# The first gathering layer of a four-layer graph network: 16 row buffers, one-hot tables three pairs ahead, group sums in pairs of one bank, the block stage over two parts

## The reference, cut to what matters

```python
x = _layernorm(x + _L0_gnn_ref(x, src, dst, edge_weight, kernel, bias))   # weighted scatter
x = _layernorm(x + _L1_gnn_ref(x, bases, weights, src, dst, edge_type_64)) # the layer of this change
x = _layernorm(x + _L2_gnn_ref(x, edge_index, edge_type_2, ...))          # 2 edge types
x = _layernorm(x + _L3_gnn_ref(x, edge_index, W1, b1, W2, b2))            # 2 convolutions

def _L1_gnn_ref(x, bases, weights, source, target, edge_type):
    xs = x[source]
    alpha = weights[edge_type]                     # 8 numbers an edge
    m = sum(alpha[:, b:b+1] * (xs @ bases[b]) for b in range(8))
    return segment_sum(m, target, num_segments=6250)
```

## Time and profile before

| what | us |
|---|---|
| median of 3 runs | 4323.59 |
| lowest and highest | 4319.92, 4335.91 |
| span of the profiled execution | 4355.4 |
| of it pass 1, first gather to last product | 1264.1 |
| busy in pass 1: PE, DVE, POOL, ACT | 780.9, 538.6, 802.9, 112.9 |

### The profile page before, as it was taken

One profiled execution on the slowest core, in us unless ns is written; L12 is line 12 of the kernel. 1 busy time (PEld: TensorE's weight loads), 2 busy tenths in 40 slices (PEclk: granted clock), 3 DMA queues, 4 the chain that ended last, 5 costly groups with the idle time before them and its releaser, 6 DMA issues. The chain is left out here.

```text
span 4355.4 us, 78937 instructions
## 1 busy us (share of the span) xinstructions
PE 3123.5 (72%) x19042; PEld 2324.3 (53%) x19043; DVE 2245.6 (52%) x6922; ACT 1982.0 (46%) x2698; POOL 2898.9 (67%) x2439
## 2 busy tenths in 40 slices
PE   4777877777777771565666666666888887887887
PEld 3444544444444440344444444445777777887877
DVE  7877777777777775344444444444022323223223
ACT  3555565555655553000001000103666666766665
POOL 3888888888888887666666666664655553553554
PEclk7888788887888885677777777777988998998898
DMA  8555666655655657111111111112444446766665
GB/s 283 99 101 101 108 112 111 106 103 104 116 101 98 108 102 246 44 47 47 48 51 49 48 48 51 49 48 71 128 137 139 138 136 186 217 212 200 203 198 155
DMA packets 362034, 506.40 MB, mean 116 GB/s; under 512 B 58808, under 2 KB 260748, under 8 KB 361324
## 3 DMA queue, kind: packets, MB, share of 16 engines
q0 software_dynamic: 178752, 183.65, 24.5%
q1 hardware_dynamic: 130122, 230.91, 17.6%
q10 hardware_dynamic: 52898, 89.11, 5.6%
HBM read 336.75 MB, written 170.10 MB: 116 GB/s over the span
## 5 line engine op out<-in xcount | busy, mean ns | idle before, releaser
L978 POOL DMA_INDIRECT rows<-t,idx_ring x1184 | 1141.7, 964 | 716.1 <-issue 329.3
L1686 PE MATMUL bank<-arena 128*128 128x384 bf16 (+1 forms) x2496 | 682.0, 409 | 397.5 <-DVE arena L2374 300.1
L1022 POOL DMA_INDIRECT sums<-rows,idx_ring x416 | 666.7, 1603 | 143.5 <-issue 115.1
L1022 POOL DMA_INDIRECT sums<-stage,idx_ring x416 | 667.2, 1604 | 126.9 <-issue 100.4
L1553 PE MATMUL bank<-planes,x_sides 128*128 128x256 f32 x3920 | 578.9, 302 | 72.2 <-issue 58.9
L978 POOL DMA_INDIRECT rows<-xp,idx_ring x384 | 373.3, 972 | 376.7 <-DMA xp<-alpha 114.3
L1553 PEld LDWEIGHTS bank<-planes,x_sides 128*128 128x128 f32 x3920 | 528.1, 204 | 84.5 <-issue 74.0
L1424 PE MATMUL bank<-S,rows 128*128 128x192 f32 x1664 | 514.4, 446 | 0.6 <-issue 0.6
L1121 ACT ACTIVATE node_data<-bank,most_sb 128x408 f32 x720 | 391.4, 602 | 229.5 <-PE bank L1689 201.5
L1686 PEld LDWEIGHTS bank<-arena 128*128 128x128 bf16 x2496 | 174.6, 109 | 599.6 <-issue 452.4
L2373 DVE TENSOR_SCALAR arena<-S 128x1176 bf16<-128x1176 int16 x832 | 450.0, 541 | 0.5 <-issue 0.5
(11 more groups left out here) (266 smaller groups left out, 5083.6 us busy)
## 6 DMA issues: line engine op xcount, KB each, us to landing
adj<-node_data ACTq DMA_DIRECT2D x112, 448.0 KB
rows<-adj SPq DMA_DIRECT2D x102, 448.0 KB
bases_sb<-adj SPq DMA_DIRECT2D x65, 448.0 KB
arena<-src SPq DMA_DIRECT2D x104, 256.0 KB
rows<-t,idx_ring POOLq DMA_INDIRECT x1184
adj_even<-node_data ACTq DMA_DIRECT2D x77, 224.0 KB
S<-adj SPq DMA_DIRECT2D x36, 448.0 KB
arena<-type SPq DMA_DIRECT2D x52, 256.0 KB
```

What stands on the lines that cost most here:

```text
L978: nc.gpsimd.indirect_dma_start(out=(part_rows if p > 2 else rows)[:, k, t, :], out_offset=None, in_=row_tables[p], in_offset=bass.Indirect ...
L1022: nc.gpsimd.indirect_dma_start(out=sums_t[t], out_offset=bass.IndirectOffsetOnAxis(ap=idx4[:, k, t:t + 1], axis=0), in_=msg[k][:, t, :], i ...
L1686: nc.tensor.matmul(bank[bk][:, 0:(hb - ha) * W], lo, hw_hot[n * GT + t][:, ha * W:hb * W], start=t == 0, stop=False)
```

## The change

In pass 1 only:

- **Rows.** The ring has 16 buffers: the old eight (`rows`) for the first body of a part and eight in `shared` (`rows_late`) for the second. POOL waits for the products of group g−16. `idx_ring` still holds two bodies and is copied where it was.
- **One-hot tables.** Four `S` buffers, made three pairs ahead.
- **Sums.** Two groups share a bank, so that four banks hold eight groups. PE waits for a free bank and DVE for the products once a pair (for the pair's second group).
- **Stage.** `base_piece` moves from pair 0 to pair 3, `add_piece` from pair 2 to pair 4. The stage takes two parts: TURN and RESIDUAL at pair 6 and NORM at pair 7 of the part three later, TURN_ROWS at pair 2 and PROJECT and TABLE at pair 4 of the part after that. The last steps of half-block NH−3 move behind the loop.
- **Around it.** The first two typed loads move from ahead of the pass to behind its last product; ACT's turning of them is split over TURN and NORM of the last half-block. `x1_back` is folded into `stored0`.

```diff
 PRODUCTS_AHEAD = RING
+ROWS_AHEAD = 2 * RING
 ADDED_AHEAD = 2
 SUM_RING = (0, 1, 3, 6)
+SUM_SLOTS = 2 * len(SUM_RING)
+S1_RING, S1_AHEAD = 4, 3
 
 STEPS = 17
 HSTEPS = BPH * RING // 2
 TURN, RESIDUAL, NORM, TURN_ROWS, PROJECT, TABLE = 5, 6, 7, 8, 10, 11
...
-PLACES = {1: {3: (TURN,), 4: (RESIDUAL,), 5: (NORM,), 6: (TURN_ROWS,), 7: (PROJECT, TABLE, REST, MID, LOW)},
-          2: {}}
-PIECE_DONE, PIECE_ADDED = 0, 2
+FIRST_HALF = {6: (TURN, RESIDUAL), 7: (NORM,)}
+SECOND_HALF = {2: (TURN_ROWS,), 4: (PROJECT, TABLE)}
+PIECE_DONE, PIECE_ADDED = 3, 4
 HB = -(-N // P)
 HW_COLS = HB * W
...
+        S_of = [S[:, 0, :, :], S[:, 1, :, :], late_S[:, 0, :, :], late_S[:, 1, :, :]]
+        rows_late = shared[:, :, :, :, :].rearrange("p e s t f -> p (e s t f)").rearrange("p (k t f) -> p k t f", k=RING, t=GT)
+        rows1 = (rows, rows_late)
+        assert len(S_of) == S1_RING == PAIRS and SUM_SLOTS == RING
         rows4 = rows[:, :, :, :].rearrange("p (s h) t f -> p s (h t) f", h=FHALF)
         sel = [shared[:, 0, s, :, :] for s in range(2)]
...
 
-        def sums_bank(k):
-
-            return bank[SUM_RING[k % len(SUM_RING)]]
+        def sums_at(k):
+
+            return bank[SUM_RING[k // 2]][:, k % 2 * (NB * W):(k % 2 + 1) * (NB * W)]
 
         def count_at(k):
 
-            return sums_bank(k)[0:2, BC - W:BC]
+            at = BC - (2 - k % 2) * W
+            return bank[SUM_RING[k // 2]][0:2, at:at + W]
 
         def parts_of(e, k, part):
...
 
             sp.wait_ge(adj_stored, 16 * NPC * (NCHUNK + 1))
             sp.wait_ge(ohot_ready, NG)
-            for m in range(2):
-                load_typed(m)
             with sp.Fori(0, NH - 2) as b:
                 sp.wait_ge(rows_ready[1], b + 2)
                 sp.dma_start(half_rows(t2_pairs, b), hst[1][0][:, 0:HALF * 2 * P].rearrange(
                     "p (c f) -> p c f", c=HALF)).then_inc(stored[1], 16)
+            sp.wait_ge(products[1], ROWS_AHEAD + NG)
+            for m in range(2):
+                load_typed(m)
             sp.wait_ge(based, NPT)
             for m in range(2, PIECES2):
...
-                                    out=(part_rows if p > 2 else rows)[:, k, t, :], out_offset=None, in_=row_tables[p],
+                                    out=(part_rows if p > 2 else rows1[j] if p == 1 else rows)[:, k, t, :], out_offset=None,
+                                    in_=row_tables[p],
                                     in_offset=bass.IndirectOffsetOnAxis(ap=idx_ring[:, j, k, t:t + 1], axis=0),
-                                ).then_inc(gathered[k], 16)
+                                ).then_inc((gathered1[j] if p == 1 else gathered)[k], 16)
 
             def gather_general(p, flag):
...
 
-                if b == NH - 3 and at == TURN_ROWS:
-                    act.wait_ge(s_ready[1], NBODY * PAIRS + 1)
-                    turn_units(0, 4)
+                if b == NH - 1 and at == TURN:
+                    act.wait_ge(s_ready[1], NBODY * PAIRS + S1_AHEAD)
+                    act.wait_ge(products[1], ROWS_AHEAD + NG)
+                    turn_units(0, 2)
+                elif b == NH - 1 and at == NORM:
+                    turn_units(2, 4)
                 elif b == NH - 1 and at == TURN_ROWS:
                     act.wait_ge(rows_ready[1], NH)
...
 
-            def group_products(i, k):
+            def group_products(m, j, k):
+                i = m * BPH + j
                 g = i * RING + k
-                pe.wait_ge(gathered[k], i * (16 * GT) + 16 * GT)
+                pe.wait_ge(gathered1[j][k], m * (16 * GT) + (past1[j][k] + 16 * GT))
                 if k % PAIR == 0:
                     pe.wait_ge(s_ready[1], i * PAIRS + (k // PAIR + 1))
-                of_pair = S[:, k // PAIR % 2, k % PAIR * GT:(k % PAIR + 1) * GT, :]
-                pe.wait_ge(added[1], g + 1)
+                of_pair = S_of[k // PAIR][:, k % PAIR * GT:(k % PAIR + 1) * GT, :]
+                if k % PAIR == 0:
+                    pe.wait_ge(added[1], g + PAIR)
                 for t in range(GT):
                     nc.tensor.matmul(count_at(k), ty2[:, bass.ds(g * GT + t, 1), :].rearrange("p e t -> p (e t)"),
-                                     S01b[:, k // PAIR % 2, k % PAIR * GT + t, :], start=t == 0, stop=t == GT - 1)
+                                     S01b[:, k // PAIR, k % PAIR * GT + t, :], start=t == 0, stop=t == GT - 1)
                 for t in range(GT):
-                    last = nc.tensor.matmul(sums_bank(k)[:, 0:NB * W], rows[:, k, t, :], of_pair[:, t, :],
+                    last = nc.tensor.matmul(sums_at(k), rows1[j][:, k, t, :], of_pair[:, t, :],
                                             start=t == 0, stop=t == GT - 1)
                 last.then_inc(products[1], 1)
...
                 at = pe.value_load(part_i[0:1, bass.ds(q, 1)], min_val=0, max_val=PIECE)
-                pe.wait_ge(added[1], q * GPH + (GPH + len(SUM_RING)))
+                pe.wait_ge(added[1], q * GPH + (GPH + SUM_SLOTS))
                 pe.wait_ge(based_added, q + 1)
...
-            def part_products(p, m, whole, first=False):
+            def part_products(m, first=False, half=False, whole=False):
 
                 for j in range(BPH):
                     for k in range(RING):
-                        group_products(m * BPH + j, k)
+                        group_products(m, j, k)
                         at = (j * RING + k) // 2
                         if k % 2 == 1:
-                            if p == 1 and at == PIECE_DONE and not first:
+                            if at == PIECE_DONE and not first:
                                 base_piece(m - 1)
                             if whole:
-                                for step in PLACES[p].get(at, ()):
-                                    stage_step(p, m - LAG, 0, step)
+                                for step in SECOND_HALF.get(at, ()):
+                                    stage_step(1, m - (LAG + 1), 0, step)
+                            if half or whole:
+                                for step in FIRST_HALF.get(at, ()):
+                                    stage_step(1, m - LAG, 0, step)
 
             def summed_piece(p, n):
...
 
-            def pass_products(p):
-                part_products(p, 0, False, True)
+            def pass_products():
+                part_products(0, first=True)
                 with pe.Fori(1, LAG) as m:
-                    part_products(p, m, False)
-                with pe.Fori(LAG, NPT) as m:
-                    part_products(p, m, True)
-                if p == 1:
-                    base_piece(NPT - 1)
+                    part_products(m)
+                part_products(LAG, half=True)
+                with pe.Fori(LAG + 1, NPT) as m:
+                    part_products(m, whole=True)
+                base_piece(NPT - 1)
+                for step in (TURN_ROWS, PROJECT):
+                    stage_step(1, NH - 3, 0, step)
                 for at in range(STEPS):
-                    stage_step(p, NH - 2, 0, at)
-                    stage_step(p, NH - 1, 1, at)
+                    stage_step(1, NH - 2, 0, at)
+                    stage_step(1, NH - 1, 1, at)
                     if at == PROJECT:
                         self_product(NH - 2, 0)
...
             def make_S(n, k):
 
-                dve.wait_ge(products[1], n * PAIR + (PRODUCTS_AHEAD - PAIR))
...
 
-                dve.wait_ge(products[1], g + (PRODUCTS_AHEAD + 1))
-                dve.wait_ge(added[1], g + len(SUM_RING))
+                if k % PAIR == 0:
+                    dve.wait_ge(products[1], g + (ROWS_AHEAD + PAIR))
+                dve.wait_ge(added[1], g + SUM_SLOTS)
                 to = G[:, :, bass.ds(at, W)]
-                sums = sums_bank(k)[:, 0:NB * W].rearrange("p (b w) -> p b w", w=W)
+                sums = sums_at(k).rearrange("p (b w) -> p b w", w=W)
                 counts = cnt_piece[:, bass.ds(at, W)]
                 nc.vector.tensor_tensor(counts, counts, count_at(k), ALU.add)
...
                 for h in range(PAIRS):
-                    make_S(i * PAIRS + (h + 1), (h + 1) % 2)
+                    make_S(i * PAIRS + (h + S1_AHEAD), (h + S1_AHEAD) % S1_RING)
                     for n in range(PAIR):
                         add_sums(i * RING + (h * PAIR + n), h * PAIR + n, ats[h * PAIR + n])
                     between(j * PAIRS + h)
 
             def start_pass():
                 copy_idx(1, 0, 0)
-                make_S(0, 0)
+                for n in range(S1_AHEAD):
+                    make_S(n, n)
 
             def start_parts(p, body):
...
```

More of the change, by code:

```diff
@@ L464, in gnn_program @@
         src_0 = bank[1][:, 4 * P - BODY:4 * P]
-        S01 = bank[5][:, 0:2 * PT * W].rearrange("p (k t w) -> p k t w", k=2, t=PT)
+        S01 = bank[5][:, 0:S1_RING * PT * W].rearrange("p (k t w) -> p k t w", k=S1_RING, t=PT)
         edges_in = sem("edges_in")
@@ L514, in gnn_program @@
         scattered = [sem(f"scattered{k}") for k in range(NTAB)]
```

(41 more changed lines are left out.)

17 lines of the change are left out of this document (9 added, 8 removed).

## The result

| | before | changed |
|---|---|---|
| median, us | 4325.26 (4 runs) | 4554.93 (4 runs) |
| lowest to highest | 4319.92 to 4335.91 | 4548.04 to 4562.4 |
| ratio | | 1.0528, 95% interval 1.0507 to 1.0548 |

The account below looks back on a forecast made before the run. It took pass 1 to be bound by PE's posts held during POOL's gather runs, which buffer stalls end. Rows +114, stage 0 and tail +7 gave +121 on 4355.4, 4476, less 31.8: 4445 us, range 4200 to 4550.

Parts of the forecast that it names:

- The rule of the held posts: Pass 1: PE's posts are on time about 7.5 to 8.8 us into a gather run, then held until 2.2 to 3.2 after.
- R1: Rival, pass 1: POOL at its pitch throughout, 40.5 us a part, 4119 us; chance 0.14.
- Left are 0 to 2 pairs: Pass 1, after a POOL run: DVE still has 0 to 2 pairs of its body to add, 0 to 5.6 us.
- runs of at least one body: Pass 1: with 16 buffers POOL's runs last at least 16 gathers, 20.2 us, instead of 12, 15.2 us, or fewer.
- the signs of being right: Expected profile: gather runs of 16 or 32, stalls 4 to 16 us, adds 2 to 3 us behind each run.
- the term of the rows: Pass 1, deeper row ring: 53 us a part instead of 48.6 over 26 parts, +114 us; bounds −21 and +270.
- my formula: Pass 1, a body: 20.2 + 2.8 + 0.9 + (0 to 5.6) us, so 47.8 to 59.0 a part, middle 53.4.
- The base: Whole kernel: profiled execution of 4355.4 us, to which the terms were added, with the median taken 31.8 us below.
- Stage and tables at 0: Pass 1: moving the stage over two parts costs 0, since PE and DVE idle 18.6 and 27.9 us a part.
- Tail +7: Behind pass 1: typed loads start at the last product, casts about 6 us later; +7 us, bounds 0 and 13.
- R2: Rival, pass 1: enough posts come through inside POOL's runs, 44.5 us a part, 4224 us; chance 0.14.
- R4: Rival, pass 1: DVE always two pairs short and stage hops add, 59 us a part, 4600 us; chance 0.06.

Follow-up runs that it names:

- e15: Changed kernel with POOL's wait depth stepped through 16, 8, 6, 4 and 3 groups within pass 1; chip 6, with the hold: 4361.3 us beside 4327.6.
- e18: Kernel before with the 16 row buffers alone and the later typed loads they need; chip 12, with the hold: 4554.62 us, ratio 1.0524.
- e17: Changed kernel with eight row buffers, typed loads and ACT's turning back where they were; chip 12, with the hold: 4322.57 us, ratio 0.9988.
- e6: Kernel before, unchanged, run again for its profile on chip 8, without the hold: 3881.52 us (one run).
- e5: Changed kernel as it is, run again on chip 3, without the hold: 3882.52 us, ratio 1.0001 to the kernel before.
- e7: Changed kernel plus a useless 3.3 MB device-memory copy once a part of pass 1; chip 8, without the hold: 3902.25 us, ratio 1.0053.
- e10: Changed kernel with PE starting each body only when its last rows have landed; chip 13, with the hold: 4581.57 us, ratio 1.0542.
- e16: Changed kernel with eight row buffers, typed loads and ACT's turning back where they were; chip 10, without the hold: 3884.64 us, ratio 1.0007.

## Why the prediction was right in sign and short in size

**The rule of the held posts** gave the right direction where the hold exists. Twice the depth made longer runs and longer holds (e15, e18), and R1 failed there: POOL did not run at its pitch, although PE and DVE had as little to do as R1 said. As a description it was too narrow: not only posts are late, PE's and DVE's own instructions are too (e17). A sign of that stood in the rows: of the 262.3 us that I gave to PE's wait for tables, 29.5 had no releaser, for 1.9 in e6. And the rule was read as one of the kernel, which was wrong: the forecast has its right sign only because the result came from a chip with the hold. On five other chips the posts are on time, POOL runs at 1.26 us a gather, and the change is worth 1.0001 (e5, on chip 3). R1's 40.5 us a part is what both kernels do there, the one before too; so even there the change brings nothing, since eight buffers had never been short without the hold. The Trainium skill ("SBUF — State Buffer", Who interferes with whom) says of the ports into SBUF that PE and ACT never wait on anyone. I had taken that as speaking for R1, but it speaks of ports alone: PE's matmuls 2.1 to 2.8 us apart in the run of 32 would go against it only if a port held them, and no run here shows what does.

**The step that failed** is "Left are 0 to 2 pairs": the prediction prices "runs of at least one body" as runs of exactly one, after which DVE has two pairs left at most. It names runs of 32 itself among the signs of being right, but no term of the sum has them. In the steady part of the trace about every second part is one run of 32. Behind a run of 32 a whole body is left, four pairs, 13.84 us (11.2 at my 2.80 a pair), and the posts come 5.3 us after the end, where I took 2.8 from runs of 12 and 24. The stall is 20.17 us for my 3.7 to 9.3. The two stalls after runs of 16 were inside these bounds (4.95, 8.72). So the part of two runs of 16 took 53.5 us (2301.46 to 2354.99), my 53, and the part of one run of 32 took 60.2. The mean of the cycle is 56.9 us, the pass 56.4: 26 x 3.4 = 88 us, which is what the term of the rows lacks (114 for 202). The upper end of my formula, 59.0, lay nearer to the 57.1 of e18, which has runs of 16 alone, than its middle. I went a little below the middle for posts that come through inside a run; in the run of 32 shown above none did: from 2367.4 to 2400.29 DVE has the index copy and one table and no add.

**The base.** The forecast was a difference of 121 us, the measured one is 230. Of the 109 that lack, 88 are the step above and 1 the tail; the pass starts 3 us sooner and the later passes are 11 us shorter in the new profile (1334.7 for 1345.6); and 33 are the base: the profiles differ by 197.0 us, the medians by 229.7. I took the 48.6 us a part from a long execution of the kernel before, and then took 31.8 us off the sum as if the changed kernel's median lay as far below its span too. It lies 2.5 us above. Where in the profile of before its surplus of some 30 us stands is open.

**Stage and tables at 0:** right, e17 0.9988 (0.9973 to 1.0003). **Tail +7:** 8.3 with the hold. Without it the same distance is 28.8 us in e5 for 21.3 in e6, +7.4; in the time of the whole only 0.9 us shows (e5, medians 3882.52 and 3881.67), since the pass starts 2.0 us sooner in e5 and differences of a few us can't be told. My way to the 7 was wrong, so that the 7 fits is luck: the casts start 14 us behind the last product, not 6. **R2 to R4:** R4 (59 a part) was nearer than the forecast; R2's posts that slip through did not come.

**Open.** What the hold is. It goes with the chip, or with the visit, and with POOL's runs of gathers; busy DMA engines did not make it where it was absent (e7); it reaches the issue of PE's and DVE's own instructions. One rival is untested: that no post is late by itself, and that the engines, slow in everything while POOL issues, act on it late. What differs between the chips no trace here tells.

## What to carry to other kernels

Before a ring is made deeper, ask what ends the wait that it is to hide. A wait that lasts as long as the producer runs grows with the depth, and here the short ring's stall was what ended it. (That depth covers a delay of fixed length is the usual reason for it; e10 was to show it and could not, since the hold was there.) When the cost of a stall is added up, price every length of run that the waits allow, the longest too. And a trace is one chip: a wait that no row explains, and that two engines leave in the same instant, is a reason to run the kernel before on other chips before any design is built on it.

## What the runs showed of the hardware that I had not expected

- The same program takes about 3881 us on chips 2, 3, 5, 8 and 10, and 4328 to 4345 on 6, 12 and 13 (11.5 to 12% more). Pass 1 is 1052 us for 1264, and the rest from pass 2's first product 1078 for 1346 (3879.7 − 2801.4 in e6; 4355.4 − 3009.8 before). Pass 0, with its scatters, takes the same: pass 1's first gather is issued at 1727.4 us in e6 and at 1726.5 before.
- The hold reaches PE's issue, with single matmuls 2.1 to 2.8 us apart in a run of 32 gathers, and DVE's: 421.6 us of idle time with no releaser in e17, 52.6 in e16, the same program on chips 12 and 10. The adds go on 3.0 us after a run of 16 (e18) and 5.3 us after one of 32.
